# Attention scores: the queries' remainder multiplied in 64-row matmuls on opposite halves of the array

## What is computed

```python
x = x + gnn(layernorm(x), edges)                      # two SAGE convolutions
# in the layer: three attentions, T = 1250, 8 heads of 64
att = softmax(q @ k.T)                                # spatial expert, no mask
att = softmax(where(causal, q @ k.T / 8, -inf))       # temporal expert, masked
att = softmax(q @ k.T)                                # cross attention, no mask
o   = att @ v                                         # each of the three
x = x + fused;  x = x + gelu(layernorm(x) @ w1.T) @ w2.T
```

## Time and profile before

| | us |
|---|---|
| median of 3 timed runs | 2041.15 (2038.39 to 2045.59) |
| the profiled execution | 2036.2 |
| its span, first to last instruction | 2034.4 |
| PE busy / DVE busy / ACT busy / POOL busy | 1761.0 / 1345.2 / 945.2 / 645.1 |
| mean granted TensorE clock | 0.956 of full speed |

### The profile page before, as it was taken

One profiled execution on the slowest core, in us unless ns is written; L12 is line 12 of the kernel. 1 busy time (PEld: TensorE's weight loads), 2 busy tenths in 40 slices (PEclk: granted clock), 3 DMA queues, 4 the chain that ended last, 5 costly groups with the idle time before them and its releaser, 6 DMA issues.

```text
span 2034.4 us, 30869 instructions
## 1 busy us (share of the span) xinstructions
PE 1761.0 (87%) x10056; PEld 1430.9 (70%) x10056; DVE 1345.2 (66%) x2744; ACT 945.2 (46%) x2146; POOL 645.1 (32%) x410
## 2 busy tenths in 40 slices
PE   2776989769999999998978787898999999789998
PEld 1554866448788888776867666777878887577776
DVE  8997124530799999831188888617999999863233
ACT  3874221221577777712156565415777777411000
POOL 4022010033434324022453524134344228143321
PEclk9988989869999999998989999999999999989999
DMA  3000000133021112033212124030211120011011
GB/s 95 6 22 22 0 26 15 67 113 72 9 43 27 25 25 57 1 102 116 63 26 47 31 44 144 13 70 1 52 26 26 25 81 23 15 42 42 31 36 55
DMA packets 32997, 88.30 MB, mean 43 GB/s; under 512 B 5191, under 2 KB 5661, under 8 KB 32370
## 3 DMA queue, kind: packets, MB, share of 16 engines
q1 hardware_dynamic: 32881, 86.83, 15.7%
HBM read 43.29 MB, written 12.80 MB: 28 GB/s over the span
## 4 chain that ended last, share of the span: by engine, by line
PE 57%; DVE 26%; issue 8%; ACT 3%; DMA 2%; POOL 2%; DVEq 1%; SPq 1%; ACTq 0%; POOLq 0%
PE ps L526 10%; PE ps L527 10%; PE ps L528 9%; PE ps L700 6%; PE ps L673 6%; PE ps L683 6%; DVE R L1327 6%; DVE ngm L1318 5%; PE ps L674 4%; DVE F L1211 3%; DVE TB L1339 2%; PE ps L622 2%; PE ps L708 1%; PE ps L623 1%; DVE rs L1336 1%
## 5 line engine op out<-in xcount | busy, mean ns | idle before, releaser
L850 ACT ACTIVATE F<-ps,ngm 125x512 f32<-125x512 f32 (+1 forms) x448 | 329.3, 743 | 135.8 <-DVE ngm L1318 130.7
L862 ACT ACTIVATE R<-ps 125x500 fp32r<-125x500 f32 (+3 forms) x624 | 279.4, 513 | 188.9 <-PE ps L683 188.7
L427 POOL TENSOR_TENSOR w_hi<-w_raw,zero 128x512 fp32r<-128x512 f32 x96 | 107.1, 1116 | 809.8 <-PE ps L528 620.6
L1327 DVE TENSOR_TENSOR R<-ps,R 125x500 fp32r<-125x500 f32 (+3 forms) x624 | 326.5, 573 | 5.1 <-ACT R L862 4.3
L1318 DVE TENSOR_REDUCE ngm<-ps 125x1 f32<-125x1250 f32 (+5 forms) x240 | 302.7, 1262 | 26.9 <-PE ps L674 23.7
L673 PE MATMUL ps<-R 128*125 128x512 f32 (+4 forms) x624 | 256.6, 411 | 70.4 <-DVE R L1327 65.6
L700 PE MATMUL ps<-R 125*128 125x252 f32 (+1 forms) x2080 | 300.9, 289 | 9.2 <-DVE F L1348 8.8
L683 PE MATMUL ps<-ident,F 125*125 125x125 f32 x2040 | 273.1, 278 | 6.6 <-ACT F L850 6.3
L700 PEld LDWEIGHTS ps<-R 125*128 125x128 f32 x2080 | 261.7, 191 | 12.5 <-issue 7.6
L683 PEld LDWEIGHTS ps<-ident,F 125*125 125x125 f32 x2040 | 250.7, 192 | 11.5 <-ACT F L850 10.0
L427 POOL TENSOR_TENSOR R<-R,zero 128x1250 fp32r<-128x1250 f32 (+1 forms) x48 | 109.0, 2270 | 454.1 <-DMA R<-F 449.3
(11 more groups left out here) (160 smaller groups left out, 2665.5 us busy)
## 6 DMA issues: line engine op xcount, KB each, us to landing
R<-F SPq DMA_DIRECT2D x96, 312.5 KB, 5.2
w_raw<-in_weights SPq DMA_DIRECT2D x96, 256.0 KB, 2.6
TB<-in_x SPq DMA_DIRECT2D x10, 250.0 KB
x_d<-F SPq DMA_DIRECT2D x10, 250.0 KB
zt_d<-F SPq DMA_DIRECT2D x1, 2500.0 KB, 8.6
F<-zt_d SPq DMA_DIRECT2D x1, 2500.0 KB, 12.2
qc_d<-F SPq DMA_DIRECT2D x4, 625.0 KB, 3.6
xt_d<-F SPq DMA_DIRECT2D x4, 625.0 KB, 3.4
```

The costliest lines, as they stand in the source:

```text
L427: return eng.tensor_tensor(to, a, zero[0:to.shape[0], :].to_broadcast(list(to.shape)), ALU.add)
L850: eng.activation(PB[0:P, n % 2, lo:hi], flat(n % 2)[0:P, lo:hi], ACT.Exp, bias=ngm[0:P, n % 2:n % 2 + 1], accum_out=rs[0:P, p, n % 4:n % 4 ...
L862: eng.activation(PT[0][:, g % 2, 4 * bank:4 * bank + nb, n % 2, 0:P], ps[0:P, 3 * (n % 2) + bank, 0:P * nb].rearrange("p (c t) -> p c t", ...
L1327: eng.tensor_tensor(PT[1][blk], ps[0:P, 3 * (n % 2) + bank, 0:P * nb].rearrange("p (c t) -> p c t", c=nb), PT[0][blk].bitcast(F32), ALU.su ...
```

## The change

`KT` becomes two tiles, one for each head b, so that the rounded keys stay in partitions 64 to 127 as long as the head is worked on. The second tile lies in a part of `R` that nothing else uses at that time. POOL's operations and their order stay.

In `scores` the main matmul L673 stays as it is. The matmul with the queries' remainder takes 64 rows instead of 128: `QSL[b][0:64] x KS[b][0:64]` for banks 0 and 2, and `QSL[b][64:128] x KT[b][64:128]` for bank 1, in both cases the rounded keys alone; the product of the two remainders is no longer computed. The order in a tile with three banks was main 0, remainder 0, main 1, remainder 1, main 2, remainder 2. It becomes main 0, main 1, remainder 0, remainder 1, main 2, remainder 2. The waits for the banks stand, as before, ahead of the main matmuls. A tile with one bank keeps its order.

```diff
-        KT = R[:, HB + 10060:HB + 10060 + 1250]
+        KT = [R[:, HB + 10060:HB + 10060 + 1250], R[:, HB + 11310:HB + 12560]]
...
-                        eng.tensor_tensor(KT[64:128, :], KS[b][64:128, :].bitcast(F32),
+                        eng.tensor_tensor(KT[b][64:128, :], KS[b][64:128, :].bitcast(F32),
...
+                q = slice(P * i, P * i + P)
+                spans = []
                 for c, (lo, w) in enumerate(CHUNKS):
-                    if lo >= K.cols[i]:
-                        continue
-                    w = min(w, K.cols[i] - lo)
-                    w += w % 2
+                    if lo < K.cols[i]:
+                        w = min(w, K.cols[i] - lo)
+                        spans.append((c, lo, w + w % 2))
+
+                def fine(c, lo, w):
+
+                    half = slice(64, 128) if c == 1 else slice(0, 64)
+                    k = KT[b] if c == 1 else KS[b]
+                    return eng.matmul(flat(n % 2)[0:P, lo:lo + w], QSL[b][half, q], k[half, lo:lo + w], start=False,
+                                      stop=True)
+                for c, lo, w in spans:
                     before = min(c, K.banks[(n - 2) % NT] - 1)
                     eng.wait_ge(A.lo, K.bank(hp, n - 2, before))
-                    to = flat(n % 2)[0:P, lo:lo + w]
-                    eng.matmul(to, QSH[b][:, P * i:P * i + P], KS[b][:, lo:lo + w], start=True, stop=False)
-                    ins = eng.matmul(to, QSL[b][:, P * i:P * i + P], KS[b][:, lo:lo + w], start=False, stop=True)
+                    eng.matmul(flat(n % 2)[0:P, lo:lo + w], QSH[b][:, q], KS[b][:, lo:lo + w], start=True, stop=False)
+                    if c == 1 or len(spans) == 1:
+                        for d in spans[0:c + 1]:
+                            ins = fine(*d)
+                    elif c == 2:
+                        ins = fine(c, lo, w)
                 ins.then_inc(A.scores, 1)
```

More of the change, by code:

```diff
@@ L468, in cut_heads @@
                         eng.wait_ge(A.cut, n0 + 4)
-                        eng.tensor_tensor(KS[b][64:128, :], KS[b][64:128, :].bitcast(F32), KT[64:128, :].bitcast(F32),
+                        eng.tensor_tensor(KS[b][64:128, :], KS[b][64:128, :].bitcast(F32), KT[b][64:128, :].bitcast(F32),
                                           ALU.subtract).then_inc(A.cut, 1)
```

## The result

The changed kernel takes 2158.56 us (median of 4 runs, 2150.31 to 2168.08), the kernel before 2042.57 (4 runs): the ratio is 1.0571, 95% interval 1.0522 to 1.062. That is 116 us more; the forecast was 92 more, 2133 against 2041. The direction held and the time lies in the range; a fifth of the loss was not foreseen.

What follows compares the result with a forecast made beforehand. PE was taken to bound the kernel, with DVE nearly as tight and bounding beside POOL. 77 us in the two unmasked stages and 15 in the masked one made 92: 2133 us against 2041, range 2055 to 2190.

Steps and rivals of the forecast that it cites:

- The price of a crossing: TensorE going between whole-array and 64-row matmuls: .19 us each time, as start .09 late plus exposed load .10.
- The free: Rival for the 64-row matmuls: crossing costs nothing, 64-row loads are taken ahead like any other; 2034 us, chance .16.
- the cheap: Rival for the 64-row matmuls: the .09 is lost at a crossing but the load is hidden; 2080 us, chance .12.
- the dear crossing: Rival for the 64-row matmuls: a crossing costs .27 us; 2183 us, chance .08.
- Running beside each other: Remainders of banks 0 and 1 in opposite array halves: .15 us saved, bounds 0 and .23.
- The quiet pair: Two neighbouring three-bank query tiles while POOL is quiet, 7.85 us: 1.26 us longer, three such pairs per ten tiles.
- The pairs beside POOL: Two pairs per ten tiles while POOL cuts heads, where DVE bounds: .53 us longer each.
- B: The tile of a pair without the normalisers' sums before its scores; beside POOL, its later scores were to cost nothing.
- The masked stage: Attention with the mask: 15 us longer, bounds 0 and 35, from about 2.5 us a head if DVE waits for all.

Runs made afterwards that it cites:

- e3: The changed kernel with the order of the kernel before, each remainder with 64 rows: six crossings in a three-bank tile, no overlap; 2251.50 us, ratio 1.1084.
- e2: The changed kernel with both remainders in the lower half of the array, so nothing runs beside; 2186.66 us, ratio 1.0728 to the kernel before.
- e1: The changed kernel's order, but every remainder matmul keeps 128 rows, so no 64-row matmul; 2076.28 us, ratio 1.0189 to the kernel before.
- the four profiles above: Masked stage of the changed kernel, twice: 289.5 and 295.2 us; with an extra matmul in masked one-bank tiles, twice: 278.9 and 286.2 us.
- e10: The kernel before with the ones that spread the normalisers (L708) 72 columns wide instead of 64; 2023.07 us, ratio 0.9928.
- e4: The changed kernel with all main matmuls of a tile first, then all remainders with 64 rows, two crossings a tile; 2111.26 us, ratio 1.0368.

## Why the forecast was right in direction and a fifth too small

- *The price of a crossing*, .19, taken from L708 and L644, held to the hundredth for rows: .42 against .23 and .30 against .11 in e3. The free, the cheap and the dear crossing fell. The Trainium skill, TensorEngine Tiling (Array Packing), Key Properties, says that changing the tiling mode drains TensorE, and was the only hint that rows would behave like columns; the trace agrees, with .19 lost at each change.
- *Running beside each other*: I took .15, by each load waiting for the other. In the trace the loads overlap as well, two remainders last 0.49, and e2 prices the overlap at .23. The Trainium skill, TensorE: Matmul & The Clock Gate, The mechanism, gives starts about 4 ns apart in different row groups; the trace agrees, with 3 to 4 ns, and my choice of .15 was too careful.
- *The quiet pair*: +1.26 foreseen, +1.10 measured (8.94 less 7.84). The .16 of difference are the two overlaps. Over 48 such pairs the sum was 8 us too high here.
- *The pairs beside POOL*: +.53 foreseen, and this is the term that failed. In an inner head of the full kernels the loss is 6.1 us (48.3 less 42.2); three quiet pairs take 3.3 of it, which leaves 1.4 for each of the two others. I took the one pair of the earlier trace rows for both pairs beside POOL. Such a second pair pays nothing at full clock (9.25 and 9.23), less than I gave it. But the first pays 1.9 (9.61 and 11.48), because POOL's cuts meet DVE's operations at other places once the tiles shift (e1 shows the same without a crossing), the third pays .4 beyond a quiet pair's 1.10, and where the clock falls in the second, that one pays .5 to 2 after all. What made DVE late in B was POOL, and I took that for slack. Two such pairs in 16 heads are 28 us more than foreseen; less the 8 of the quiet pairs that is 20 too few, and with the 77 it gives 97, where 99 were measured.
- *The masked stage*: 15 foreseen, 27.5 measured. DVE waits for scores 20 us longer there. The 2.5 us a head of crossings are 20 if all of them show, and the clock went from 0.93 to 0.82. Inside my bounds (35). At full clock a masked head pays 1.0 to 1.5 us, less than the 1.9 that I took (15 / 8); the rest goes with the clock, which I had only as a remark.
- The timed runs agree with the account: an estimated 97 us at full clock, where 16 heads x 5.5 and 8 masked heads x 1.0 to 1.5 give 96 to 100, and 19 to 24 with the clock.
- That the total came out as near as it did is in part luck: the quiet pairs' surplus (8 us) hid part of what was missing beside POOL (28) and under the mask (12).

What stays open is why the clock falls, and with it how firm the masked stage's shares are: by the four profiles above each microsecond at half clock costs it about .18, which would make some 12 of 27.5; by the three heads at full clock some 16 to 19.

## What to carry to other kernels

Price a change of the array's shape before using part of it: here .19 us in and .19 us out, each about the time in which 450 columns stream (the 286 columns between 226 and 512 take .12), so that one pair of 512-column matmuls beside each other (.23 saved) does not pay for the two crossings around it (.38). By these numbers two pairs in one block would (.46), an estimate that no run here tests. And look for matmuls that cross unasked: 72 columns of ones instead of 64 took 0.7% off the kernel before. And idle time that another engine's interference has made is no slack: shift the work, and the interference falls elsewhere.

## What the runs showed of the hardware

- Two 64-row matmuls in opposite halves, with their loads, run fully beside each other: both start within 3 to 4 ns, and the next whole-array matmul follows .42 us later, as after a single one (e3).
- A crossing between whole-array and 64-row or 64-column matmuls costs .19 us in both directions: .42 instead of .23 after 512 columns, .30 instead of .11 after 226 (e3); the load at it is not hidden. With 72 stationary columns instead of 64 the crossing is gone (e10).
- A DVE operation on 2 columns (L1348, before L1336) takes 0.15 us where POOL is quiet. Where it meets a tensor-tensor operation of POOL it ends .02 us after that one, and so takes up to 2.2 us (before, changed, e1, e4, in every such case); beside POOL's tensor-scalar operations it mostly stays at 0.15. The DVE operations that read PSUM (L1330, L1339) keep their durations.
- Mean granted clock and time go together within one kernel: .24 to .26 us for each microsecond at half clock (10 and 14 executions).
